# Three issuers for the first stack transfers, and slot reads ahead of weight loads, in an attention and expert kernel

## The chip, the core and the metric

The kernel runs on one core of a Trainium2 chip. The core has five engines with queues of their own: TensorE (PE, with its weight loads shown as PEld), VectorE (DVE), ScalarE (ACT), GpSimd (POOL) and SyncE (SP), which here only issues DMAs. ACT and POOL issue DMAs too. The metric is the device time of one execution in microseconds (us), as the median of several runs.

## What is computed

A gated cross-attention layer, then a mixture of experts in which each token goes to one expert. Batch 4, 512 tokens, width 256, 16 heads of 16; 8 experts of width 1024. All in float32.

```python
def xattn(query, ctx, adj, mask, Wq, bq, ...):        # heads of 16
    scores = einsum('bhqd,bhkd->bhqk', Q, K) / sqrt(16) + adj
    scores = where(mask == 0, -inf, scores)
    out = einsum('bhqk,bhkd->bhqd', softmax(scores), V)
    return out @ Wo.T + bo

x = x + tanh(g_xattn) * xattn(layernorm(x), ctx, ...)
n = layernorm(x)
e = argmax(softmax(n @ gate_w.T))                     # one expert a token
x = x + tanh(g_ffn) * prob[e] * (relu(n @ w1[e] + b1[e]) @ w2[e] + b2[e])
```

## The kernel before, in words

**Attention.** The four batches run one after the other, each in 64 score tiles of 128 queries by 512 keys for one head. `step(b, n)` exists once for each engine, and step n does a little for several tiles: PE makes the scores of tile n (L940); DVE adds the mask and takes the row maximum (L1588); POOL (L682) or, for two of eight tiles and a few at the end, ACT (L1255) negates and shifts; PE transposes tile n-4 (L951); ACT exponentiates it (L1229); PE weighs the values (L963). Score tiles use three PSUM banks (`NS`), their results six SBUF buffers (`NB`), the transposes two PSUM banks (`NTB`). The other work (projections of the next batch, tail of the batch before: heads, turn, out, normed, gate, rank) is dealt to fixed steps by lists such as `LAST_USES`, `SLOT_STEPS` and `TABLE_STEPS`.

**The stack.** Q and K are split into three bf16 parts each, and the eight products that matter are stacked along the partitions, so one bf16 matmul gives a score. `stack_in` (L348 to L356) copies from `parts` into the stack: for each half g and side t (0 is Q, 1 is K), eight DMAs of 64 KB. In batch 0 the stack comes in four groups, m by g, and scores of tiles 0, 8, 16, 24 wait for groups 0 to 3 (`s_first`). SP issues most of them (L400 to L407), ACT five and three of the t=1 ones of groups 0 and 1 (`FIRST_ACT`). While they are under way PE runs filler matmuls (`keep_busy`, L820): 46, then a wait for `s_issued` (SP is through group 0), then 12. All engines work their own queue in order.

**Last batch.** Most tokens' experts are known before the last batch ends, so five "early" slots of 128 tokens are prepared in it. DVE builds a slot table in twelve pieces at `TABLE_STEPS` (expert of a slot in `eid`, its start in `base_i`), POOL writes token numbers to `slot_d` in DRAM (L644). SP then loads the weights w1 of three slots (`early_w1`, L484), waits for POOL's writes and reads the five slots' token lists (L497), then two w2 matrices, rows, and two w2 more. POOL copies the lists (`early_index`, L652) at `INDEX_STEP` and gathers token rows with indirect DMAs: `early_normed(s)` (L658) for the normalised ones, of which slots 0 and 1 at `NORMED_STEPS`, and `early_x(s)` (L665) for the residual ones. A wait in front of them holds up POOL's shifts (L682) behind. After the last step POOL issues the other gathers; PE turns rows (L1029), multiplies w1 (L1041) and w2 (L1063), the first use of w2 waiting for all eight matrices (`r_w2`).

**Late slots.** The other slots run in a loop (L1104, L1127, L1137), after which the kernel ends.

Of the kernel before, what the change touches and what calls it, by code (L numbers as in the profile page):

```python
# [11 lines left out]
ds = bass.ds  # L12
# [10 lines left out]
PAIRS = sum(K_PARTS)  # L23


def build(nc, x, ctx_in, mask, g_xattn, g_ffn, adj, Wq, bq, Wk, bk, Wv, bv, Wo, bo,
# [14 lines left out]
    EARLY = -(-(KNOWN - X * (P - 1)) // P)  # L41
# [7 lines left out]
    NG = H // HG  # L49
# [3 lines left out]
    TPG = QPG * HG  # L53
    TILES = GROUPS * TPG
# [3 lines left out]
    NQ = P // (HG * D)  # L58
# [7 lines left out]
    LP = LE + 1  # L66
    LO = LP + QT
    LAG = LO + 1
    FIRST_ACT = (5, 3, 0, 0)
    ACT_SHIFTS = (3, 6)  # L70
    LAST_ACT_SHIFTS = (60, 63)

# [57 lines left out]
                  if w in ("next q", "next k")}  # L130
    SPLIT_STEPS = {n + 1: use for n, use in CAST_STEPS.items()}
    SLOT_STEPS, SCATTERED_STEP = ((54, 59, 62, 67), (41, 43, 46, 47)), (73, 60)
    TABLE_STEPS = (41, 42, 43, 44, 45, 48, 49, 50, 51, 52, 65, 66)
    INDEX_STEP, NORMED_STEPS = TILES - 5, (TILES - 5, TILES - 2)
    ABS_STEPS = {29: 0, 34: 1, 40: 2, 45: 3}
    SHUT_STEPS = {31: 0, 36: 1, 44: 2, 48: 3}
    FIRST_ABS_STEPS, FIRST_SHUT_STEPS = {1: 2, 4: 3}, {2: 2, 5: 3}
# [27 lines left out]
    with ExitStack() as st:  # L165
# [3 lines left out]
        def sem(name):  # L169
            return st.enter_context(nc.semaphore(name))  # L170
# [79 lines left out]
        least, done, stepd = (sb(n, [P, X]) for n in ("least", "done", "stepd"))  # L250
# [44 lines left out]
        t_x, t_out = ([sem(f"{n}{k}") for k in range(2)] for n in ("t_xres", "t_out"))  # L295
        s_adj, s_perm, s_issued = sem("adj"), sem("perm"), sem("issued")
        s_first = [sem(f"first{g}") for g in range(NG)]
        r_fill, r_filled = sem("r_fill"), sem("r_filled")
        s_eps, t_eps, s_half = sem("eps"), sem("t_eps"), sem("half")
        s_md = [sem("md0"), sem("md1")]  # L300
# [37 lines left out]
            eng.sem_inc(s_waited[eng is nc.vector], 1)  # L338

        FIRST = 16 * 2 * PAIRS  # L340
        STACKED = NQ * FIRST

        def place_of(h):
# [4 lines left out]
        def stack_in(eng, par, t, g, m0, m1, ranks, done):  # L348

            pairs = [(q, k) for q, n in enumerate(K_PARTS) for k in range(n)]  # L350
            for rank in ranks:
                a = pairs[rank][t]
                eng.dma_start(
                    stack[rank:P:PAIRS, par, t, g * HG * EC:(g + 1) * HG * EC].rearrange(
                        "p o (h m) s -> p (o h) m s", m=EC)[:, :, m0:m1].rearrange("p h m s -> p h (m s)"),
                    parts[g * (P // NQ):(g + 1) * (P // NQ), t, a, m0:m1].rearrange("p m s -> p (m s)")).then_inc(done, 16)  # L356
# [15 lines left out]
        def _(sp):  # L372
# [27 lines left out]
            for m in range(EC):  # L400
                for g in range(NQ):
                    for t in range(2):
                        sp.wait_ge(s_parts, 2 * m + t + 1)
                        stack_in(sp, ds(0, 1), t, g, m, m + 1, range(FIRST_ACT[m * NQ + g] if t == 1 else 0, PAIRS),
                                 s_first[m * NQ + g])
                    if (m, g) == (0, 0):
                        sp.sem_inc(s_issued, 1)  # L407
# [42 lines left out]
            for b in range(B - 1):  # L450
                t, par = b * QT, ds((b + 1) % 2, 1)
# [32 lines left out]
            def early_w1(s):  # L484
                u = s % len(ew1)
                e = sp.value_load(eid[0:1, s:s + 1], min_val=0, max_val=X - 1)
                sp.dma_start(ew1[u], w1_v[ds(e, 1)].rearrange("x p k f -> p (x k) f")).then_inc(e_w1[u], 16)

            sp.wait_ge(s_stack, last * STACKED)
            sp.wait_ge(e_eid, 1)  # L490
            sp.wait_ge(s_xT, B * 4)
            for s in range(3):
                early_w1(s)
            sp.wait_ge(r_scat, B * (16 * QT))
            for s in range(EARLY):
                at = sp.value_load(base_i[0:1, s:s + 1], min_val=0, max_val=X * TOK)
                sp.dma_start(slots[:, s], slot_d[ds(at, P), 0:2]).then_inc(e_slots, 16)  # L497
            sp.wait_ge(s_score, last * TILES + 6 * TILES // 8)
            for e in range(X // 2, X, 2):
                load_w2(e)  # L500
# [50 lines left out]
        def _(po):  # L551
# [9 lines left out]
            def norm(b):  # L561
                wait_apart(po, s_mv, b * QT + QT)
                po.tensor_scalar(mv[:, :, 1], mv[:, :, 1], EPS, None, ALU.add).then_inc(s_eps, 1)
                po.wait_ge(s_eps, b + 1)
                po.tensor_tensor(rstd[:], mv[:, :, 1], minus_half[:], ALU.pow).then_inc(s_rstd, 1)
# [10 lines left out]
            n = 5  # L576
# [29 lines left out]
            def mask(b, qt):  # L606

                wait_apart(po, s_penal, b * QT + qt + 1)
                po.tensor_tensor(adjm[:, qt], adjr[:, qt], maski[:, qt].bitcast(F32), ALU.subtract  # L609
                                 ).then_inc(s_adjm, 1)  # L610
# [11 lines left out]
            po.wait_ge(s_adj, 16)  # L622
            for qt in range(QT // 2):
                mask(0, qt)
            norm(1)

            def tail_rstd(b, k):
# [30 lines left out]
            def early_normed(s):  # L658
                if s >= EROWS:
                    wait_apart(po, f_xt, s - EROWS + 1)  # L660
                po.indirect_dma_start(erow[s % EROWS][1], None, xn_d[0:KNOWN],  # L661
                                      bass.IndirectOffsetOnAxis(ap=eidx[:, s:s + 1], axis=0)
                                      ).then_inc(e_row[s % EROWS], 16)

            def early_x(s):  # L665
                if s >= EROWS:
                    wait_apart(po, f_out, s - EROWS + 1)
                po.indirect_dma_start(erow[s % EROWS][0], None, x1_d[0:KNOWN],
                                      bass.IndirectOffsetOnAxis(ap=eidx[:, s:s + 1], axis=0)
                                      ).then_inc(e_x1[s % EROWS], 16)  # L670
# [61 lines left out]
            early_x(0)  # L732
            wait_apart(po, s_osb, B * GROUPS + 2)
            early_normed(3)
            early_x(1)
            early_normed(4)
            early_x(2)
            pairs(B, B)
            for t in range(*RANKED[0]):
                to_slots(t)  # L740
            for k in range(2):
                tail_rstd(B, k)
            for s in range(3, EARLY):
                early_x(s)
            pairs(B, B + 1)
            for t in range(*RANKED[1]):
# [50 lines left out]
        def _(pe):  # L797
# [19 lines left out]
            def keep_busy(n, o=bank[0]):  # L817

                for _ in range(n):
                    pe.matmul(o[:, 0:2 * P], ones[:], ident[:].bitcast(BF16), start=True, stop=True)  # L820
# [148 lines left out]
            def step(b, n, uses, last=False):  # L969

                if n < TILES or not last:
                    if n < NG * TPG and n % TPG == 0 and b == 0:
                        pe.wait_ge(s_first[n // TPG], FIRST)
                    if n == TILES:

                        pe.wait_ge(s_stack, b * STACKED + STACKED)
                    scores(b, ds((b + n // TILES) % 2, 1), n)
                if LT <= n and (n < TILES + LT or not last):
                    transposes(b, n - LT)
                if n >= LP + TPG and (n - LP) % TPG in (0, 2):  # L980
                    g, c = divmod(n - LP - TPG, TPG)
                    if g == 0 and c == 0:
                        pe.wait_ge(s_v, b * 2 + 2)
                    weigh(b, g, c)
                    weigh(b, g, c + 1)
                for i, what, k in at_step(uses, n - 1):
                    if what.startswith("next"):
                        next_rest(b, i, what, k)
                for i, what, k in at_step(uses, n):
                    if what == "heads" and k == 2:  # L990

                        pe.wait_ge(s_osb, b * GROUPS + (NG + 2))
                    if what == "values":
                        values(b, i, k)
                    elif what.startswith("next"):
                        next_use(b, i, what, k, b + 1)
                    else:
                        tail_use(b, i, what, k)
# [3 lines left out]
                next_use(0, first_next(j), what, k, 0)  # L1002
                next_rest(0, first_next(j), what, k)
            pe.wait_ge(s_parts, 2)
            keep_busy(46)
            pe.wait_ge(s_issued, 1)
            keep_busy(12)
            pe.wait_ge(t_ones, 2)
# [143 lines left out]
        def _(act):  # L1152
# [25 lines left out]
            def next_use(b, i, what, k, nxt):  # L1178
                o = sp_bank[i % 2]
                act.wait_ge(s_m, ready(b, i))  # L1180
                if what in ("next x", "next ctx"):
                    dst = xT if what == "next x" else cT
                    act.activation(dst[:, k], o[:], ACT.Copy).then_inc(s_xT, 1)
                    act.wait_ge(s_xT, nxt * 4 + (1 if what == "next x" else 3) + k)
                    act.sem_inc(s_md[i % 2], 1)
                else:
                    t = int(what == "next k")
                    if nxt == 1:
                        for g in range(NG):
                            act.wait_ge(s_first[g], FIRST)  # L1190
                    if nxt > 1:
                        act.wait_ge(s_stack, (nxt - 1) * STACKED)
                    act.activation(parts[:, t, 0, k], o[:], ACT.Identity,
                                   bias=(bqc, bkc)[t][:, k:k + 1]).then_inc(s_p0, 1)
# [619 lines left out]
```

## Time and profile before

| | us |
|---|---|
| median of 3 runs | 548.91 |
| lowest, highest | 548.83, 552.67 |
| the profiled execution: time | 550.53 |
| the profiled execution: span, first to last instruction | 548.5 |
| PE busy | 526.3 |
| DVE, ACT, POOL busy | 302.3, 309.1, 297.9 |

The granted TensorE clock is 0.998 of full over the span. Busy time is a sum over the span; whether an engine's work sets the end must be read from the waits of the stretch in question. Times in the rows below count from the span's first instruction.

### The profile page before, as it was taken

The page shows a single profiled execution, that of the slowest core. Times are in us where ns is not written, and L with a number is a line of the kernel's source. Part 1 is how long each engine was busy: PE and PEld are TensorE (multiplying, and loading weights), DVE is VectorE, ACT ScalarE, POOL GpSimd, SP SyncE. Part 2 cuts the span into 40 slices and gives each one's busy share as a digit, 9 for nine tenths or more (in the row PEclk, how much of TensorE's full clock was granted, in tenths as well). Part 3 has the DMA queues.
Part 4 walks back from the last instruction along what each step waited for, and adds up shares of the span by engine and source line. Part 5 has one row for each costly group of instructions (what it writes and reads, how often), then busy time and mean ns, then how long its engine had stood idle before and what let it go on. Part 6 is the DMA issues. An engine that isn't in the chain of part 4 may idle for free. (4 is left out here: it accounts for less than half of the span.)

```text
span 548.5 us, 13306 instructions
## 1 busy us (share of the span) xinstructions
PE 526.3 (96%) x4123; PEld 405.1 (74%) x4124; DVE 302.3 (55%) x923; ACT 309.1 (56%) x678; POOL 297.9 (54%) x424
## 2 busy tenths in 40 slices
PE   8999999989999999999999999888999999999997
PEld 5577667667666667666676666658899999999996
DVE  2776587976677887668885878845340211111111
ACT  4366678665678665778675676664332333333322
POOL 5346566665567575468574556555244444443451
PEclk9999999999999999999999999999999999999999
DMA  8633625400405510204520057499136665555570
GB/s 288 206 110 132 192 65 183 149 31 6 150 21 192 166 50 1 79 10 153 180 85 1 11 184 250 147 362 320 59 103 218 211 205 196 178 187 184 189 210 1
DMA packets 51489, 77.67 MB, mean 142 GB/s; under 512 B 9945, under 2 KB 34601, under 8 KB 51305
## 3 DMA queue, kind: packets, MB, share of 16 engines
q1 hardware_dynamic: 46600, 67.72, 37.0%
q0 software_dynamic: 4192, 8.73, 5.0%
q8 instruction: 29, 0.48, 0.4%
q10 hardware_dynamic: 640, 0.52, 0.3%
q14 instruction: 28, 0.22, 0.1%
HBM read 52.76 MB, written 8.35 MB: 111 GB/s over the span
## 5 line engine op out<-in xcount | busy, mean ns | idle before, releaser
L1588 DVE CUSTOM_DVE_ANT_0 prob<-bank,adjm 128x512 f32<-128x512 f32 x256 | 172.3, 688 | 70.6 <-issue 39.9
L1229 ACT ACTIVATE pt<-bank 128x512 f32<-128x512 f32 x256 | 152.1, 596 | 87.7 <-PE bank L951 81.2
L682 POOL TENSOR_SCALAR prob<-prob,negmax 128x512 f32<-128x512 f32 x190 | 132.0, 698 | 117.6 <-DVE negmax L1588 113.4
L951 PE MATMUL bank<-ident,prob 128*128 128x128 f32 x1024 | 154.8, 274 | 2.2 <-POOL prob L682 1.3
L951 PEld LDWEIGHTS bank<-ident,prob 128*128 128x128 f32 x1024 | 124.2, 141 | 39.7 <-issue 13.7
L1299 ACT ACTIVATE adjm<-bank,colsm 128x128 f32<-128x128 f32 x184 | 52.6, 368 | 105.0 <-PE bank L1127 80.0
L940 PE MATMUL bank<-w2s 128*128 128x512 bf16 x256 | 97.5, 381 | 8.5 <-DVE negmax L1588 5.7
L963 PE MATMUL bank<-pt,vals 128*32 128x256 f32 x1024 | 68.3, 385 | 0.9 <-DVE vals L1386 0.5
L1127 PEld LDWEIGHTS bank<-xT,pt 128*128 128x128 f32 x576 | 67.1, 192 | 0.9
L1127 PE MATMUL bank<-xT,pt 128*128 128x128 f32 x576 | 67.2, 275 | 0.0
L1137 PE MATMUL bank<-w2s,adjm 128*128 x288 | 65.1, 379 | 0.0
L1137 PEld LDWEIGHTS bank<-w2s,adjm 128*128 128x128 f32 x288 | 53.3, 190 | 6.5
L1255 ACT ACTIVATE prob<-prob,negmax 128x512 f32<-128x512 f32 x66 | 47.4, 719 | 13.7 <-DVE negmax L1588 12.3
L1783 DVE SCALAR_TENSOR_TENSOR cT<-bank,slots,rows 128x256 f32<-128x256 f32 x18 | 8.7, 484 | 72.5 <-PE bank L1137 72.4
L940 PEld LDWEIGHTS bank<-w2s 128*128 128x128 bf16 x256 | 25.5, 100 | 31.3 <-DVE negmax L1588 14.9
L963 PEld LDWEIGHTS bank<-pt,vals 128*32 128x32 f32 x1024 | 27.0, 109 | 22.7 <-issue 9.8
L644 POOL DMA_INDIRECT slot_d<-pair,posi x20 | 20.9, 1046 | 19.3 <-DVE posi L1511 10.0
L1776 DVE SCALAR_TENSOR_TENSOR rows<-maski,slots,rows 128x256 f32<-128x256 f32 x18 | 8.7, 484 | 39.8 <-DMA rows<-x_d,lidx 27.9
L753 POOL COPY lidx<-slots 128x1 int32<-128x1 int32 x18 | 5.1, 283 | 43.4 <-DMA slots<-slot_d 43.2
L767 POOL DMA_INDIRECT out_y<-cT,lidx x18 | 18.3, 1015 | 15.9 <-DVE cT L1783 11.0
L755 POOL DMA_INDIRECT rows<-xn_d,lidx x18 | 18.1, 1005 | 14.3 <-POOL lidx L753 12.7
L609 POOL TENSOR_TENSOR adjm<-adjr,maski 128x512 f32<-128x512 f32 x16 | 20.6, 1285 | 3.1 <-ACT maski L1218 3.1
(195 smaller groups left out, 624.4 us busy)
## 6 DMA issues: line engine op xcount, KB each, us to landing
pt<-in_L_ffn_w SPq DMA_DIRECT2D x19, 1024.0 KB
w2s<-parts SPq DMA_DIRECT2D x96, 128.0 KB
w2s<-in_L_ffn_w SPq DMA_DIRECT2D x8, 1024.0 KB
maski<-in_mask_Bx1xSxS_ik SPq DMA_DIRECT2D x4, 1024.0 KB, 5.6
w2s<-parts SPq DMA_DIRECT2D x56, 64.0 KB, 2.1
xres<-in_x SPq DMA_DIRECT2D x18, 128.0 KB
x_d<-rows SPq DMA_DIRECT2D x18, 128.0 KB
xn_d<-rows SPq DMA_DIRECT2D x18, 128.0 KB
```

The costliest lines, as they stand in the source:

```text
L609: po.tensor_tensor(adjm[:, qt], adjr[:, qt], maski[:, qt].bitcast(F32), ALU.subtract).then_inc(s_adjm, 1)
L644: po.indirect_dma_start(slot_d, bass.IndirectOffsetOnAxis(ap=posi[:, t:t + 1], axis=0), pair[:, t], None, bounds_check=X * TOK - 1, oob_is ...
L682: po.tensor_scalar(prob[:, m], prob[:, m], -1.0, negmax[:, m:m + 1], ALU.mult, ALU.add).then_inc(s_shpool, 1)
L940: pe.matmul(sc_bank[m][:], q, k, start=True, stop=True).then_inc(s_score, 1)
L951: mm = pe.transpose(tr_bank[n % NTB][:, c * P:(c + 1) * P], prob[:, n % TILES % NB, c * P:(c + 1) * P], ident[:])
L963: mm = pe.matmul(pv_bank[32 * j:32 * j + 32, (g % 2) * HALF:(g % 2 + 1) * HALF], vals[:, c, hg * HG + j, :], pt[:, g % 2, c, j, :], start= ...
L1127: mm = pe.matmul(h_bank(u, c), w1s[:, v, k, c * P:(c + 1) * P], xgT[:, u, k], start=k == 0, stop=k == EC - 1)
L1137: mm = pe.matmul(y_bank(u), hT[:, u, c], w2s[:, ds(e, 1), c, :].rearrange("p x e -> p (x e)"), start=c == 0, stop=c == FC - 1)
L1229: act.activation(pt[:, g % 2, :, j, q2 * P:(q2 + 1) * P], tr_bank[c % NTB][:].rearrange("p (c q) -> p c q", c=QT), ACT.Exp).then_inc(s_cac ...
L1255: act.activation(prob[:, m], prob[:, m], ACT.Identity, scale=-1.0, bias=negmax[:, m:m + 1]).then_inc(s_shact, 1)
L1299: act.activation(hT[:, u, c], h_bank(u, c), ACT.Relu, bias=b1c[:, ds(e * FC + c, 1)]).then_inc(f_hT, 1)
L1588: ve.tensor_tensor_reduce(out=prob[:, m % NB], in0=sc_bank[m % NS][:], in1=adjm[:, qt], scale=-1.0, scalar=BIG, op0=ALU.add, op1=ALU.min, ...
```

## The change

`FIRST_POOL = 3`: of group 0's eight t=1 transfers ACT issues 4 (was 5), POOL 3 with a semaphore of its own, and SP 1 (was 3). The first `keep_busy` goes from 46 to 36. In the last batch SP reads the five slots ahead of the three w1 loads. `INDEX_STEP` is one step earlier (58 for 59), the first five `TABLE_STEPS` one later. After the last step POOL gathers `early_normed(4)` ahead of `early_x(1)`, and `early_x(2)` comes behind the two `tail_rstd`.

```diff
-    FIRST_ACT = (5, 3, 0, 0)
+    FIRST_ACT = (4, 3, 0, 0)
+    FIRST_POOL = 3
...
-    TABLE_STEPS = (41, 42, 43, 44, 45, 48, 49, 50, 51, 52, 65, 66)
-    INDEX_STEP, NORMED_STEPS = TILES - 5, (TILES - 5, TILES - 2)
+    TABLE_STEPS = (42, 43, 44, 45, 46, 48, 49, 50, 51, 52, 65, 66)
+    INDEX_STEP, NORMED_STEPS = TILES - 6, (TILES - 5, TILES - 2)
...
+        s_fpool = sem("fpool")
...
+        FIRSTS = [FIRST - 16 * FIRST_POOL] + [FIRST] * (NG - 1)
...
-                        stack_in(sp, ds(0, 1), t, g, m, m + 1, range(FIRST_ACT[m * NQ + g] if t == 1 else 0, PAIRS),
+                        done = FIRST_ACT[m * NQ + g] + (FIRST_POOL if (m, g) == (0, 0) else 0)
+                        stack_in(sp, ds(0, 1), t, g, m, m + 1, range(done if t == 1 else 0, PAIRS),
                                  s_first[m * NQ + g])
...
             sp.wait_ge(s_xT, B * 4)
-            for s in range(3):
-                early_w1(s)
             sp.wait_ge(r_scat, B * (16 * QT))
             for s in range(EARLY):
                 at = sp.value_load(base_i[0:1, s:s + 1], min_val=0, max_val=X * TOK)
                 sp.dma_start(slots[:, s], slot_d[ds(at, P), 0:2]).then_inc(e_slots, 16)
+            for s in range(3):
+                early_w1(s)
...
             for qt in range(QT // 2):
                 mask(0, qt)
+            po.wait_ge(s_parts, 2)
+            stack_in(po, ds(0, 1), 1, 0, 0, 1, range(FIRST_ACT[0], FIRST_ACT[0] + FIRST_POOL), s_fpool)
             norm(1)
...
             early_normed(3)
+            early_normed(4)
             early_x(1)
-            early_normed(4)
-            early_x(2)
             pairs(B, B)
...
-            for s in range(3, EARLY):
+            for s in range(2, EARLY):
                 early_x(s)
...
-                        pe.wait_ge(s_first[n // TPG], FIRST)
+                        pe.wait_ge(s_first[n // TPG], FIRSTS[n // TPG])
+                        if n // TPG == 0:
+                            pe.wait_ge(s_fpool, 16 * FIRST_POOL)
...
             pe.wait_ge(s_parts, 2)
-            keep_busy(46)
+            keep_busy(36)
             pe.wait_ge(s_issued, 1)
             keep_busy(12)
...
-                            act.wait_ge(s_first[g], FIRST)
+                            act.wait_ge(s_first[g], FIRSTS[g])
+                        act.wait_ge(s_fpool, 16 * FIRST_POOL)
```

## Rows read from the trace of the kernel before

**Rows 1.** The page, busy time: us, share of the span, instructions
```profile
PE 526.3 (96%) x4123; PEld 405.1 (74%) x4124; DVE 302.3 (55%) x923; ACT 309.1 (56%) x678; POOL 297.9 (54%) x424
```

**Rows 2.** Windows: stretch, length, busy by engine, clock, DMA share, GB/s
```profile
13.00:20.00 7.00, 6.77 (x16) 2.78 (x16) 3.75 (x6) 5.20 (x9) 3.62 (x5) 1.00 0.82 265
20.00:26.00 6.00, 5.85 (x48) 4.50 (x48) 4.81 (x12) 0.63 (x1) 0.63 (x2) 1.00 0.50 158
...
412.00:545.00 133.00, 132.18 (x906) 124.19 (x906) 18.34 (x38) 46.17 (x162) 57.98 (x70) 1.00 0.54 183
```

**Rows 3.** Timeline to group 1: start, us, engine (q: DMA issue), operation, idle before
```profile
23.80 3.17 SPq L353 DMA_DIRECT2D w2s<-parts  x5
...
20.97 4.35 ACTq L353 DMA_DIRECT2D w2s<-parts  x5
...
21.00 6.50 PE L820 MATMUL bank<-ident,ones 128*128 128x256 bf16 x58 [0.15 <-DVE parts L1669]
...
21.83 0.43 DVE L1667 CAST parts<-rest 128x512 bf16<-128x512 f32 x1
...
25.76 0.24 POOL L563 TENSOR_SCALAR mv<-mv 128x4 f32<-128x4 f32 x1 [5.37 <-DVE mv L1363]
...
27.35 0.38 PE L940 MATMUL bank<-w2s 128*128 128x512 bf16 x1
...
35.58 0.39 PE L940 MATMUL bank<-w2s 128*128 128x512 bf16 x1 [0.91 <-DMA w2s<-parts]
```

**Rows 4.** DMA issues, 12 to 34 and 38 to 46: KB each, us to landing
```profile
w2s<-parts SPq DMA_DIRECT2D x24, 64.0 KB, 2.2
...
xn_d<-atT POOLq DMA_DIRECT2D x1, 1.0 KB, 8.3
...
slot_d<-rows POOLq DMA_DIRECT2D x1, 512.0 KB, 3.2
```

**Rows 5.** Timeline of the last batch near tiles 42 and 48, DVE and PE
```profile
334.42 0.56 DVE L1511 TENSOR_SCALAR posi<-posf,dead 128x4 int32<-128x4 f32 x1
...
335.57 0.69 DVE L1588 CUSTOM_DVE_ANT_0 prob<-bank,adjm 128x512 f32<-128x512 f32 x1 [0.21 <-DVE cmp_t L1531]
...
336.33 0.39 PE L940 MATMUL bank<-w2s 128*128 128x512 bf16 x1 [1.10 <-DVE negmax L1588]
...
344.71 0.39 PE L940 MATMUL bank<-w2s 128*128 128x512 bf16 x1 [0.47 <-DVE negmax L1588]
```

**Rows 6.** Timeline of SP's queue in the last batch
```profile
349.13 0.39 SPq L487 DMA_DIRECT2D adjr<-in_L_ffn_w  x1
...
352.62 4.84 SPq L497 DMA_DIRECT2D slots<-slot_d  x5
```

**Rows 7.** Timeline at the last tiles: POOL, PE and ACT
```profile
361.44 0.19 POOL L655 COPY eidx<-slots 128x5 int32<-128x5 int32 x1 [1.25 <-DMA slots<-slot_d]
...
364.42 0.66 PE L951 MATMUL bank<-ident,prob 128*128 128x128 f32 x4 [0.85 <-POOL prob L682]
...
364.35 0.71 ACT L1255 ACTIVATE prob<-prob,negmax 128x512 f32<-128x512 f32 x1
...
365.11 0.60 ACT L1229 ACTIVATE pt<-bank 128x512 f32<-128x512 f32 x1
```

**Rows 8.** DMA by queue (packets, MB, share) and landing, 348 to 377 us
```profile
q1 hardware_dynamic: 6676, 8.61, 88.0%
q0 software_dynamic: 257, 0.73, 6.8%
...
xcin<-in_L_ffn_w SPq DMA_DIRECT2D x1, 1024.0 KB, 8.9
```

**Rows 9.** Timeline of PE in the first experts
```profile
370.98 1.95 PE L1041 MATMUL bank<-xT,adjr 128*128 128x128 f32 x16
...
377.19 0.41 PE L919 MATMUL bank<-ident,attn 128*128 128x128 f32 x2 [1.90 <-DVE region L1503]
...
382.73 3.62 PE L1063 MATMUL bank<-w2s,adjm 128*128 x16
```

## The prediction

> **What bounds the kernel now.** I read the page first: TensorE (PE) is busy 96% of the span [rows 1]. The windows then say where the other 4% lies [rows 2]. From 412 us on PE is busy 132.2 of 133 us, so the second half of the experts can give nothing; what the change can win lies ahead of it. Two stretches bear on it: the run-up to the first score tile, where PE is "busy" mostly with filler matmuls (L820), and the last batch with the first experts, 330 to 412 us. A filler is busy time that costs what it delays, so for the run-up the timeline counts, not the share.
>
> **Run-up.** The page's chain does not reach back so far, so I read the timeline. PE runs 58 fillers from 21.00 and the first score starts at 27.35 [rows 3]; one filler is worth (27.35 - 21.00)/58 = 0.109 us. Beside them the stack transfers are issued: SP one each 3.17/5 = 0.63 us, ACT five from 20.97 to 25.32 [rows 3]. SP issues eight of t=0 and three of t=1 for group 0; the row of five SP issues in [rows 3] begins with its first t=1 transfer at 23.80, so the third starts at about 25.07 and, with 2.2 us to landing [rows 4], is there at 27.3: fillers and transfers end together. The next gate is group 1: PE idles 0.91 us until 35.58 for its transfers [rows 3]. The list of waits has no other place where PE waits for the stack.
>
> **Change 1, issuers.** Of group 0's eight t=1 transfers ACT now issues 4, POOL 3 and SP 1. SP's ninth starts at 23.80 and lands at 26.0. ACT's fifth issue goes; its fourth starts near 20.97 + 3 x 0.87 = 23.6 and lands at 25.8. POOL waits for the same semaphore, about 20.97, and has been idle for 5.37 us when its next work, the norm of batch 1, starts at 25.76 [rows 3]. No POOL issue stands in that stretch; priced as an SP issue, three end near 22.9, as an ACT issue near 23.6, and nothing is late behind them. Landing of a POOL transfer is the unknown. Rows from both sides: 2.2 us for SP's own 64 KB, 3.2 us for the 512 KB fill of slot_d from POOL, 8.3 us for a 1 KB write from POOL [rows 4], issued near 14 us when the DMA engines were 82% busy [rows 2]. From 20 to 26 us they are 50% busy [rows 2], nearer to the fill's case, so I take 3.2: third issue at 22.3, landed at 25.5.
> The trace shows that DVE's cast of 128x512 takes 0.43 us inside this window [rows 3]. The Trainium skill (SBUF — State Buffer, SBUF: two separate sides) warns that a vector operation in a two-port mode keeps GpSimd from writing the descriptors of its DMAs. By that rule the POOL transfers could slip by that cast, to 25.9 instead of 25.5; no run here shows it yet, and neither landing changes the sum.
>
> PE: 48 fillers instead of 58, so the first score at 21.00 + 48 x 0.109 = 26.25, a gain of 1.1 (the wait on s_issued passes: SP is through its ninth at 24.4, the 36th filler ends at 24.9). What counts is the group 1 gate. SP has two issues fewer ahead of group 1, so 2 x 0.63 = 1.27 us earlier: 35.58 becomes 34.31. PE would be there at 35.58 - 0.91 - 1.10 = 33.57 and waits 0.74. Groups 2 and 3 come from the same stream and move alike. Gain 1.27, carried through the batches, since PE is the bound there and waits for no stack transfer again.
>
> **Change 2, table steps.** Five pieces of the slot table move one step on. Before, the first stands ahead of tile 42 on DVE: posi ends at 334.98, the tile starts at 335.57, and PE loses 1.10 us at 336.33 [rows 5]. Without the piece the tile starts some 0.6 earlier. But all five remain ahead of tile 47, and PE's next wait is for tile 48, 0.47 us at 344.71 [rows 5]; DVE's work up to there is unchanged, so the 0.6 reappears as a longer wait there. Cost 0; bounds -0.6 and +0.3 (one more link).
>
> **Change 3, slot reads ahead of three weights.** Before: three weight loads from 349.13, five slot reads from 352.62 to 357.46, 1.12 apart with their value loads [rows 6], then two w2 loads. Swapped, the slot reads start at 349.13 ahead of all the weights' bytes and are in before 357; the weights start 5 x 1.12 = 5.6 us later, at 354.7. The w2 issues behind them stay, the same eight instructions standing ahead. The weights land late but hidden: the slowest of the three took 8.9 us [rows 8], 5.6 later it is in by 366, and PE uses the first at 370.98 [rows 9].
> POOL's early_index no longer idles 1.25 us for the slots [rows 7], and moved a step ahead, with its gather, it lets tile 61's negation on POOL run some 2 us earlier. PE's 0.85 us wait at 364.42 goes [rows 7]. Does the end of attention follow? ACT works in order: negation of tile 63 (364.35 to 365.06), then tile 61's exponential at 365.11 [rows 7], already right behind. PE's transposes of tile 63 need that exponential's bank, and the last exponential stands behind those. So only 0.05 us is won: the wait moves from tile 61's to tile 63's transposes, since the ACT negation is next in line.
>
> What is paid: the DMA stream. Between 348 and 377 us 8.61 MB move on q1 and 0.73 on q0 [rows 8]; w2 needs 3 w1, 4 w2, two xres and four row stores ahead of or with it, 8.12 MB of q1, so it is complete just before 377. PE first reads it at 382.73 [rows 9]. The stream started near 350.9 (an estimate: 1.8 us behind its first issue, a little under the 2.2 us that a small one takes to landing; rate 9.34/26.1 = 0.358 MB/us) and will start 5.6 later, 356.5. Seven gathers (0.92 MB) now fall before its end: 9.04/0.358 = 25.3, so 381.8. By plain shift, 377 + 5.6 + 0.5, 383.1. PE's need of 382.73 lies between: cost 0 to 0.4. I take 0, the byte count being the nearer reckoning. The x-row loads and stores slip by the same 5.6 and are used from 380 on.
>
> **Change 4, gathers.** early_normed(4) goes ahead of early_x(1), and early_x(2) behind tail_rstd, with some 1 us of POOL each. early_x(2) is then issued near 385 and used near 403; POOL meanwhile passes the pairs' wait, which DVE sets, no earlier. 0.
>
> Sum: -1.27 + 0 - 0.05 + 0 + 0 = -1.3 on a span of 548.5. That execution took 550.5 in all; the median of the runs is 548.9, and I set the same difference against it: 547.6.
>
> **Rivals.**
> A, forecast: 547.6, own range 547.0 to 548.2.
> B, the waits in the last batch are real gains too: PE's 0.85 and DVE's 0.6 both count, 547.6 - 1.4 = 546.2. Or the stranger 1.90 us wait at 377.19 [rows 9], in which DVE, ACT and SP all got PE's signals late in the midst of the full DMA stream, does not recur: 545.7. For it: the waits are in the rows; against the first: ACT's row right behind.
> C, w2 late: if gathers and stream slow each other, complete by 383.7 or later, 1 us or more given back, 548.6. It decides once w2 lands past 382.7; nothing lies behind it to absorb it, since PE is full to the end.
> D, the start gains nothing: three issuers slow each other. ACT's five issues beside SP's took 4.35/5 = 0.87 us each against SP's 0.63 [rows 3], so issuers do cost each other. If SP's nine lose 9 x 0.14 = 1.27 us to the third issuer, group 1 is no earlier: 548.9.
> E, the other side: POOL's transfers land late. By the 8.3 us row the third is there at 22.3 + 8.3 = 30.6. From the first score to group 1 PE needs 34.67 - 27.35 = 7.32 us, so group 1 starts at 37.9 instead of 35.58: +2.3, 551.2. It eats into the gain from a landing at 27.0 on and makes the kernel slower from 28.3. Half-way between the two rows, 5.7 us (28.0), the gain would be 0.3. The Trainium skill (DMA: Bandwidth & Descriptors, Anatomy of one DMA — SWDGE (gpsimd) path) gives about 2.0 us plus bytes/436e3, an estimate of 24.5 for this landing; the 8.3 us row here does not agree with it, the slot_d row nearly does, and by it the sum stays.
>
> **Chances.** A 0.50, B 0.18, C 0.10, D 0.12, E 0.10. The range reaches from B's far case, 545.7, toward E, which is mostly left out, with C and D inside and a little for a median of few runs: 545.7 to 549.6. About 1% (5.5 us) is what a measurement of this kernel can tell from no change; only several cases together or something unseen get there: faster 0.04, same 0.94, slower 0.02.
>
> **What would show it.** First score at 26.2 to 26.3, POOL's transfers with 3 us to landing, a shorter wait ahead of group 1 at 34.3: right. First score past 27: D or E, told apart by SP's and POOL's issue rows. A wait at PE's first L1063 matmul: C. PE's waits near tiles 45 and 48: 0.5 and 1.1 instead of 1.1 and 0.5 if step 2 is right. L951 without its 0.85 wait, but another ahead of tile 63's transposes, and the last exponential no earlier relative to tile 60's transposes: step 3. Wrong would be a gain over 2 us with all of it after 330 us.

## The result, and the profile after

In the first comparison, four runs of each kernel, the changed kernel took 555.63 us in the median (552.88 to 557.54) and the kernel before 549.31: ratio 1.0104, 95% interval 1.0073 to 1.0135. Forecast were 547.6 and a gain of 0.2%. The square brackets behind a ratio are its 95% interval from here on. Against many more runs the changed kernel came out at 1.0025 [1.0004, 1.0046] and 1.0027 [1.0005, 1.0049] in two further comparisons (12 runs against 35 each). So the sign of the loss is firm and its size is not; both figures are taken up below. The profiled execution has a span of 550.9 us, 2.4 more than before.

The page after, busy time, which answers [rows 1]:

```profile
PE 527.8 (96%) x4113; PEld 404.6 (73%) x4114; DVE 303.1 (55%) x923; ACT 308.8 (56%) x678; POOL 299.4 (54%) x427
```

The windows after (stretch, length, busy time of PE, PEld, DVE, ACT and POOL with instructions, granted clock, DMA share, GB/s), for [rows 2] and the last batch:

```profile
20.00:26.00 6.00, 5.85 (x49) 4.50 (x48) 5.25 (x13) 0.69 (x1) 2.25 (x5) 1.00 0.70 175
...
350.00:357.00 7.00, 6.68 (x55) 4.43 (x50) 6.33 (x19) 4.93 (x10) 2.79 (x5) 1.00 0.11 5
357.00:384.00 27.00, 23.86 (x204) 18.44 (x204) 13.28 (x52) 14.41 (x38) 14.08 (x20) 0.94 1.03 361
412.00:545.00 133.00, 132.08 (x907) 123.86 (x906) 17.87 (x37) 46.88 (x165) 57.29 (x70) 1.00 0.57 183
```

The same two stretches of the last batch in the kernel before:

```profile
350.00:357.00 7.00, 6.07 (x48) 3.96 (x46) 6.39 (x20) 4.49 (x8) 3.70 (x7) 1.00 0.89 311
357.00:384.00 27.00, 23.16 (x209) 18.70 (x210) 12.92 (x48) 14.10 (x37) 14.05 (x20) 1.00 0.99 339
```

From 412 us on nothing has changed. Between 350 and 357 the DMA engines, which carried 311 GB/s before, now carry 5. That hole is the slot reads' place in SP's queue, and all the weight bytes stand behind it.

**The run-up.** Timeline after, for [rows 3]:

```profile
22.62 2.16 SPq L356 DMA_DIRECT2D w2s<-parts  x2
...
22.33 2.46 ACTq L356 DMA_DIRECT2D w2s<-parts  x2
...
21.27 1.63 POOL L356 DMA_DIRECT2D w2s<-parts  x3 [0.84 <-DVE parts L1677]
...
27.71 0.38 PE L945 MATMUL bank<-w2s 128*128 128x512 bf16 x1 [1.27 <-DMA w2s<-parts]
...
34.87 0.38 PE L945 MATMUL bank<-w2s 128*128 128x512 bf16 x1
35.50 0.63 PE L956 MATMUL bank<-ident,prob 128*128 128x128 f32 x4 [0.25 <-ACT pt L1237]
```

POOL's transfers among the DMA issues of 20 to 34 us after (KB each, median us to landing), beside [rows 4]:

```profile
w2s<-parts POOLq DMA_DIRECT2D x3, 64.0 KB, 3.0
```

POOL's three issues take 1.63 us and land 3.0 us later in the median, near the 3.2 reckoned, but the third, the one that counts, takes 4.00 and is in at 26.39 instead of 25.5. Two issues of SP take 2.16 us and two of ACT 2.46. The fillers end at 26.4, and PE then idles 1.27 us for SP's ninth transfer, issued at 23.29 and landed at 27.62: 4.33 us, where the sum had 2.2. So the first score (the matmul of the first score tile) is 0.36 later than before instead of 1.1 earlier. Group 1 is no longer waited for, but right behind it PE waits for ACT (pt at 35.50).

**The last batch.** SP's queue after, for [rows 6]:

```profile
350.20 4.86 SPq L499 DMA_DIRECT2D slots<-slot_d  x5
355.83 0.40 SPq L491 DMA_DIRECT2D adjr<-in_L_ffn_w  x1
...
358.57 5.54 SPq L475 DMA_DIRECT2D w2s<-in_L_ffn_w  x2
364.15 4.14 SPq L414 DMA_DIRECT2D xres<-in_x  x2
...
370.87 3.62 SPq L475 DMA_DIRECT2D w2s<-in_L_ffn_w  x2
```

The timeline of POOL and PE, for [rows 7, 9]:

```profile
359.74 0.19 POOL L661 COPY eidx<-slots 128x5 int32<-128x5 int32 x1
...
366.02 0.63 PE L956 MATMUL bank<-ident,prob 128*128 128x128 f32 x4 [0.47 <-ACT pt L1237]
...
367.78 3.51 PE L968 MATMUL bank<-pt,vals 128*32 128x256 f32 x32 [0.20 <-issue]
...
377.29 0.41 PE L924 MATMUL bank<-ident,attn 128*128 128x128 f32 x2 [0.28 <-DVE region L1511]
...
384.12 1.13 PE L1070 MATMUL bank<-w2s,adjm 128*128 x4 [1.12 <-issue]
...
413.72 0.44 PE L1111 MATMUL bank<-ident,rows 128*128 128x128 f32 x2 [0.59 <-DMA rows<-xn_d,lidx]
```

A window of PE at the end of attention, columns as above:

```profile
368.00:371.00 3.00, 3.00 (x32) 1.63 (x24) 0.30 (x2) 0.00 (x0) 0.00 (x0) 0.50 1.09 355
```

POOL no longer waits for the slots. PE waits 1.12 us ahead of the first w2 matmul; by the landings in the trace the last w2 byte is in at 383.92, before at 377.18. The 32 matmuls that weigh the values and end attention (L968) take 3.51 us, 1.93 in the profile of e13, because the granted clock is 0.50 from 368 to 371: the 1.2 GHz level. PE had been busy but for waits of 0.2 to 0.5 us before it fell.

### The profile page after: what moved, and what is told of

Same layout as the page of the kernel before. It is cut to its first block and busy times, and to the rows that moved or that the text cites. A ratio compares the mean times of both kernels' runs of the same rounds, so it can differ in the third digit from the quotient of the medians.

```text
span 550.9 us, 13291 instructions
## 1 busy us (share of the span) xinstructions
PE 527.8 (96%) x4113; PEld 404.6 (73%) x4114; DVE 303.1 (55%) x923; ACT 308.8 (56%) x678; POOL 299.4 (54%) x427
## 5 line engine op out<-in xcount | busy, mean ns | idle before, releaser
L968 PE MATMUL bank<-pt,vals 128*32 128x256 f32 x1024 | 69.9, 392 | 0.9 <-DVE vals L1394 0.5
L945 PEld LDWEIGHTS bank<-w2s 128*128 128x128 bf16 x256 | 25.5, 100 | 31.3 <-issue 15.8
L968 PEld LDWEIGHTS bank<-pt,vals 128*32 128x32 f32 x1024 | 27.7, 110 | 23.2 <-issue 10.6
L766 POOL DMA_INDIRECT rows<-x_d,lidx x18 | 17.2, 954 | 10.0 <-DVE cT L1791 5.2
```

The costliest lines, as they stand in the source:

```text
L945: pe.matmul(sc_bank[m][:], q, k, start=True, stop=True).then_inc(s_score, 1)
L968: mm = pe.matmul(pv_bank[32 * j:32 * j + 32, (g % 2) * HALF:(g % 2 + 1) * HALF], vals[:, c, hg * HG + j, :], pt[:, g % 2, c, j, :], start= ...
```

## The experiments

Eighteen profiles of these kernels (both kernels, their repeats and the versions below) share most of their path, so steps are compared across all of them. Whole times are compared only within a set: versions that ran side by side, with runs of the kernel before among them. That matters here: the kernel before took 549.69 us in the median among e1 to e4, 553.87 among e5 to e7, 552.72 with c1 and 551.99 with c2. Where two versions of one set are compared below, the difference is of their means, and the figure behind ± is its 95% interval, worked out from the single times.

**e1: the run-up's change alone.** Kernel before with

```diff
-    FIRST_ACT = (5, 3, 0, 0)
+    FIRST_ACT = (4, 3, 0, 0)
+    FIRST_POOL = 3
...
-            keep_busy(46)
+            keep_busy(36)
```

> The kernel before with the run-up of the change alone (4 issues on ACT, 3 on POOL, 1 on SP, 36 filler matmuls). Theory S (the slot swap makes it slow): this one is no slower than before, 0 to 1 us faster: first score near 27.7 as in the changed kernel, group 1 near 34.9, no clock drop near 368, no wait at the first L1070 matmul. Theory R (the run-up is what costs): 3 to 6 us slower than before.

Measured: 1.0024 [1.0010, 1.0038]. In place of the expected gain of 0 to 1 us that is a loss of 1.3 us, much less than the 3 to 6 us of the other theory. First score 27.31, tile 8 at 34.49, but tile 16's exponential only 0.24 us earlier than before, and this profile has the clock at its lower level from 365.3 to 368.7. Over all profiles, the exponential of tile 16 starts at 52.80 to 54.43 us in the eleven kernels with three issuers (mean 53.46, standard deviation 0.50) and at 53.26 to 53.84 in the seven with two (mean 53.56, 0.19). The third issuer gains nothing that these show, and the spread is wider with it.

**e2 and e12: the slot reads ahead of the weights, alone.**

```diff
-            for s in range(3):
-                early_w1(s)
             sp.wait_ge(r_scat, B * (16 * QT))
             for s in range(EARLY):
...
+            for s in range(3):
+                early_w1(s)
```

and INDEX_STEP one earlier.

> The kernel before with the slot reads ahead of the weights and INDEX_STEP one step earlier, nothing else. Theory S: 3 to 6 us slower than before (about 1%), w2 complete near 384 us, a wait of 1 to 3 us at the first w2 matmul of the early slots, and a stretch at half clock near 365 to 372. Theory R and theory T (table steps): as before within 1 us.

> The kernel before with the slot reads ahead of the weights and the index computation one tile earlier, again, now beside the changed kernel. Theory that the slot reads are the whole loss of the change but for some 0.1%: within 0.2% of the changed kernel. Rival, that run-up and table steps add their own 0.25% each, as each showed alone: 0.3 to 0.5% below the changed kernel.

Measured: e2 1.0073 [1.0046, 1.0100], e12 1.0008 [0.9989, 1.0028] (mean 0.95 ± 1.01 us below c2, so within the expected 0.2%, with the rival's 0.3% not excluded). PE's timeline at the first w2 matmul in e2, and the window behind it:

```profile
384.69 1.70 PE L1063 MATMUL bank<-w2s,adjm 128*128 x6 [3.42 <-issue]
```

```profile
386.00:389.00 3.00, 3.00 (x9) 2.35 (x8) 0.00 (x0) 0.00 (x0) 0.00 (x0) 0.50 1.03 395
```

and the timeline of e12:

```profile
377.40 0.41 PE L919 MATMUL bank<-ident,attn 128*128 128x128 f32 x2 [1.90 <-DVE region L1503]
...
383.70 1.56 PE L1063 MATMUL bank<-w2s,adjm 128*128 x6 [0.59 <-issue]
```

w2 lands at 384.49 and 383.51, 7.3 and 6.3 us later than before. In e2 PE pays 3.42 us, and 1.7 more for the clock, which fell to the 1.2 GHz level at 386.0, after that wait. In e12 it pays 0.59: PE was already held up 1.90 us at 377.40, the wait that [rows 9] show. So how much of the late weights is felt depends on what else has delayed PE. The same edit measured 0.7% in one set and 0.1% in another; that this is the reason is argued from one profile of each.

**e3: table steps later and gathers moved.**

```diff
-    TABLE_STEPS = (41, 42, 43, 44, 45, 48,
+    TABLE_STEPS = (42, 43, 44, 45, 46, 48,
```

> The kernel before with the five table steps one later and the moved gathers, nothing else. Theory T (DVE's work near tiles 42 to 48 costs): 1 to 3 us slower, with a long DVE copy near 340. Theory S: within 0.5 us of before.

Measured: 1.0025 [1.0011, 1.0038]; e4 below, which has this edit too, 1.0013. That is the 1 to 3 us slower of the first theory. The profile has no wait for w2 (landed 378.42, needed 381.27). The exponentials of tiles 38 and 50 lie 16.69 us apart, before 16.25.

**e4: the changed kernel without the slot swap.** SP's order and INDEX_STEP as before.

> The changed kernel with the weights again ahead of the slot reads and INDEX_STEP as before. Theory S: 0 to 1 us faster than before. Theory R or T: nearly all of the changed kernel's loss of 4 to 6 us remains.

Measured: 1.0013 [0.9999, 1.0027], against 1.0073 for e2 beside it. Here w2 lands at 378.71 and PE does not wait. In this set the swap is the larger part of the loss: e2's mean is 3.6 ± 1.4 us above e4's. But e4 was not faster than before, as expected, and it holds the edits of e1 and e3 together, which measured 0.24% and 0.25% alone. So these two figures do not add up, and neither is much above what such a set can tell.

**e5 and e10: one megabyte less ahead of w2.** The changed kernel with the third early w1 transfer behind the second pair of w2:

```diff
-            for s in range(3):
+            for s in range(2):
                 early_w1(s)
...
             for e in range(X // 2 + 1, X, 2):
                 load_w2(e)
+            early_w1(2)
```

> The changed kernel with the third early weight load moved behind the second pair of w2 loads; the slot reads stay first. Theory S (w2 comes late because 3 MB of weights start 5.6 us later ahead of it): 1 MB less ahead of w2, so w2 is complete near 381 and the wait at the first w2 matmul is gone; 2 to 4 us faster than the changed kernel, within 0.3% of before. Theory Q (it is the clock or the gathers, not the order of the bytes): as slow as the changed kernel, 1.007 or more of before.

> The changed kernel with the third early first-layer transfer behind the second pair of second-layer transfers, again, now beside the changed kernel itself on one chip. Theory of the late weights: 0.7 to 1.2% below the changed kernel, and between 0.4% below and 0.1% above the kernel before. Rival, that the changed kernel loses by its run-up and table steps: within 0.3% of the changed kernel.

**c1: the changed kernel itself, beside e8 to e10.**

> The changed kernel itself once more, as the control for its neighbours on the same chip. If its loss is its own (the slot reads put 3.1 MB of first-layer weights beside the second-layer weights, which land at 383.9 us of its profile and not at 377.2): slower than the kernel before by 0.7 to 1.1% here too, and by as much than the version with the third early first-layer transfer behind the second pair of second-layer transfers. If the first comparison was a matter of that chip: within 0.3% of the kernel before.

Measured: e5 0.9969 [0.9949, 0.9989], e10 0.9984 [0.9965, 1.0003], c1 1.0025 [1.0004, 1.0046]. The mean of e10 is 552.04, of c1 554.01: 1.97 ± 0.99 us, or 0.36%, for moving one transfer. Both expectations had the changed kernel's loss at 0.7% or more, as in the first comparison; c1 shows 0.25%, within the 0.3% of its rival, and e10's gain is half of what was expected, its interval reaching into the 0.3% of the rival. The timeline of PE in c2 (the second repeat of the changed kernel; c1 waited 1.59), then in e10:

```profile
384.12 1.12 PE L1070 MATMUL bank<-w2s,adjm 128*128 x4 [1.90 <-issue]
```

```profile
381.66 1.95 PE L1049 MATMUL bank<-xT,parts 128*128 128x128 f32 x16
383.45 1.89 PE L1071 MATMUL bank<-w2s,adjm 128*128 x8
```

In e10 the w2 matmul follows without a wait; w2 is in at 381.87. Nothing else was touched, and the changed kernel is then no slower than the kernel before: this pair, with e13 and e11 below, carries the mechanism. The two profiles alone would not. Their first w2 matmuls start together (383.40 in c1, 383.45 in e10), since e10 ended attention 1.15 us later. And moving the transfer may be worth something by itself, as e9 shows next.

**e8 and e9: the same on the kernel before,** e8 with the slot swap, e9 without.

> The kernel before with the slot reads ahead of the early first-layer weights and the index computation one tile earlier, and with the third early first-layer transfer (1 MB) moved behind the second pair of second-layer transfers. Theory that the bytes ahead of the second-layer weights are the loss: those weights land 2.7 to 3 us earlier than with the slot reads alone (384.5 us), so by about 381.7, the 3.42 us wait ahead of the first second-layer matmul is gone, and the time is within 0.3% of the kernel before, against 0.73% above it for the slot reads alone. Theory that the slot reads cost by something else (the queue of SP held up, the earlier index computation): still 0.5 to 0.8% slower.

> The kernel before, with nothing but the third early first-layer transfer moved behind the second pair of second-layer transfers. Theory that in the kernel before the weights are in time as they stand (landed 377.2 us, used first at 382.73 with no wait): within 0.2% of before. If instead the lighter stream is what made two versions of the changed kernel 0.3 to 0.45% faster than before: faster by 0.3% or more here too.

Measured: e8 0.9987 [0.9967, 1.0008], e9 0.9979 [0.9955, 1.0002]. The slot swap costs nothing that the runs show once w2 is in time (380.58): e8's mean is 0.6 ± 1.0 us above e9's. And e9 has no swap and yet POOL does not wait for the slots, as its timeline shows:

```profile
359.27 0.57 POOL L633 TENSOR_TENSOR rstd<-mv,minus_half 128x1 f32<-128x1 f32 x1
359.79 0.19 POOL L656 COPY eidx<-slots 128x5 int32<-128x5 int32 x1
```

With two weight loads ahead of the slot reads instead of three, these are early enough. I had expected e9 to be equal to before within 0.2%; its point value is just there, and the interval does not tell it from a small gain. If that gain is real, a part of e10's 1.97 us could have the same source. Against it speaks that what e9's profile gains, POOL's wait for the slots, is gone in the changed kernel already, and that the waits for w2 which e10 removes (1.12 to 1.90 us in the four profiles with them) are of the size of its gain. No run separates the two.

**e7: fillers in place of the wait,** 24 of them ahead of PE's wait for w2 in the changed kernel, to keep the clock up.

> The changed kernel with 24 filler matmuls (2.6 us of PE) ahead of the wait for w2. Theory S with an idle-bound clock: the wait is filled, no half-clock stretch follows the w2 wait, mean granted clock of the runs 0.998 or more, time 0 to 1 us less than the changed kernel. If the clock falls for another reason: clocks of 0.994 to 0.996 as in the changed kernel, and time equal or up to 1.5 us more.

Measured: 0.9995 [0.9973, 1.0017]. PE's timeline:

```profile
383.04 2.78 PE L825 MATMUL bank<-ident,ones 128*128 128x256 bf16 x24
385.66 1.68 PE L1072 MATMUL bank<-w2s,adjm 128*128 x7
```

The clock stayed at 1.00 from 384 to 390, but the fillers ran 1.2 us past w2's landing (384.45), and part of the price only changed its name. The mean granted clock of its runs, 0.9984, is where it was expected, but e5 and e6 beside it, without the fillers, have 0.9976 and 0.9979. Whether e7 beats the changed kernel can't be said, since the two were not in one set. It is slower than moving the transfer: e5, beside it, is 1.4 ± 0.8 us below it.

**c0: the kernel before, a second profile.**

> The kernel before, unchanged, for a second profile. If the 1.90 us wait behind the first rank matmuls belongs to the kernel it is there again; if it was of that one execution, about 0.3 us stand there, the first w2 matmul starts near 381, and about 0.5 to 0.9 us of wait stand at the first late gather instead.

Measured: 552.69 us with a span of 550.7. The 1.90 us wait is there again (1.96), so it is not of one execution. The 2.2 us over the first profile are spread: run-up 0.25, 0.4 more to the last exponential (POOL's wait for the slots is 2.09 instead of 1.25), 0.5 between there and the late rows, and 1.0 behind the late rows.

**c2, e11, e6 and e13: what the table steps cost inside the change.** e11 is the changed kernel with the old TABLE_STEPS (five steps differ), e6 and e13 (one kernel, run twice) have the late third transfer besides.

> The changed kernel itself, a second control. If the kernel before takes 549 to 550 us on this chip, 0.7 to 1.0% above it (second-layer weights landed at 383 to 384 us, 1.1 to 1.6 us of wait, and a stretch at half the clock in some executions). If the kernel before takes 552 us or more, as in the two last sets, 0.2 to 0.4% above it, since those executions lose clock in both kernels.

> The changed kernel with nothing but the six table steps back at tiles 41 to 45. In four profiles with the steps moved and the slot reads ahead, the exponentials of tiles 38 to 50 of the last batch lie 16.94 to 16.96 us apart, in six with the old steps 16.24 to 16.28. Theory that this is on the path: those 16.25 us again, and the kernel 0.5 to 0.7 us (0.1%) faster than the changed one. Rival, that the weights land no earlier for it, so that what the tiles give back is waited out ahead of the second-layer matmuls: the wait there grows by as much, and the time is the same within 0.05%.

> As e5_w2first, and the table steps where they were before. Theory T2 (the table steps one later put a COPY on VectorE beside a slot scatter on GpSimd, +0.4 to 0.7 us between tiles 38 and 50): 0.4 to 0.7 us faster than e5_w2first, at or under before (0.998 to 1.001). If the steps cost nothing: equal to e5_w2first.

> The changed kernel with the third early first-layer transfer behind the second pair of second-layer transfers and the old table steps, the version that came out 0.45% faster than the kernel before on one chip. Theory that it is better by what its profile shows (no wait of GpSimd for the slots, 0.9 us of its path; weights in time): 0.1 to 0.4% faster than the kernel before here too, and 0.6% or more below the changed kernel. Rival, that its lead came from executions in which the kernel before lost clock: within 0.15% of the kernel before.

Measured: c2 1.0027 [1.0005, 1.0049], e11 1.0017 [0.9996, 1.0038], e6 0.9955 [0.9937, 0.9974], e13 0.9981 [0.9962, 1.0000]. Moving the transfer is seen again: e13's mean is 2.09 ± 0.93 us below e11's. The old table steps are not seen in whole times: e11 is 0.91 ± 1.15 us below c2, and e6 0.16 ± 0.83 below e5, where 0.4 to 0.7 was expected. They are seen in every trace. From tile 38's exponential to tile 50's it takes 16.94 to 16.95 us in the six profiles with the new steps and the slot swap, 16.69 and 16.72 in e3 and e4 without the swap, and 16.24 to 16.29 in the ten with the old steps. In e11 the wait for w2 is still 1.65 us, so what the tiles give back may be waited out there, as its rival had it. The timelines of DVE, PE and POOL in the changed kernel:

```profile
339.50 1.20 DVE L1549 COPY end<-end 128x2 f32<-128x2 f32 x1
...
342.02 0.42 DVE L1410 TENSOR_TENSOR attn<-bank,rinv 128x256 f32<-128x256 f32 x1
342.59 0.17 DVE L1549 COPY end<-end 128x4 f32<-128x4 f32 x1
342.79 0.16 DVE L1550 TENSOR_TENSOR end<-end 128x4 f32<-128x4 f32 x1
...
342.65 0.41 PE L924 MATMUL bank<-ident,attn 128*128 128x128 f32 x2 [0.90 <-DVEq L1414]
...
339.31 1.36 POOL L688 TENSOR_SCALAR prob<-prob,negmax 128x512 f32<-128x512 f32 x2
```

and in e11:

```profile
338.67 0.32 DVE L1549 COPY end<-end 128x2 f32<-128x2 f32 x1
...
337.99 1.02 POOL L650 DMA_INDIRECT slot_d<-pair,posi  x1 [0.17 <-issue]
339.06 0.70 POOL L688 TENSOR_SCALAR prob<-prob,negmax 128x512 f32<-128x512 f32 x1
```

A copy of two numbers a partition takes 1.20 us and ends at 340.70, as POOL's two negations end (339.31 + 1.36 = 340.67); in e11 it ends at 338.99 and POOL's instruction at 339.01. One step later, the small table operations begin just after a negation has begun. The Trainium skill (SBUF — State Buffer, SBUF: two separate sides) says that a vector operation in a two-port mode or with two SBUF inputs and a GpSimd operation take a shared pair of ports as an exclusive lock, and the later one blocks until the other's instruction ends. The trace agrees in that the copy ends within 0.03 us of an instruction of POOL in both places; whether the copy ran in such a mode it doesn't tell. By that rule one negation would have to be sat out. In the changed kernel it is two, back to back (339.31 to 340.67); in e3 the same copy takes 0.52 us and ends with the first of them. In addition a second table piece now shares a tile with rinv and attn of the row before it, so PE's transposes of attn wait.

## Why the prediction was wrong

By its own steps, on the profiled execution (span 548.5 to 550.9):

**Run-up, forecast -1.27.** Failed. POOL's landing was near (3.0 us in the median, 4.00 for the third; rival E did not occur, since 26.39 is still ahead of the 27.0 from which it would have eaten into the gain). The first score was forecast from a landing of SP's ninth transfer at 26.0; the median of 2.2 us was taken for it, and it took 4.33. For group 1, what failed is "SP has two issues fewer ahead of group 1, so 2 x 0.63 = 1.27 us earlier", in two places. ACT's and SP's issues were priced by their means, and a pair of SP's took 2.16 us and a pair of ACT's 2.46 beside a 16 KB instruction fetch that the trace shows at 23.0 to 23.9 us (in the kernel before at 22.05 to 23.4, with one issue of 1.46 on ACT and one of 1.15 on SP beside it); that is a coincidence in time, not a tested cause. And a gate that goes was taken as time won: behind it ACT's pace holds PE (the wait for pt at 35.50), so of 0.7 to 1.1 us at tile 8 there are -0.2 to +0.6 left at tile 16's exponential (six profiles: after, c2, e1, e4, e11, e13; mean 0.1). Rival D has the outcome. Its reason, three issuers slowing one another evenly, the issue times do not show, since most of SP's stay at 0.6 us; the landings of the transfers issued from 21 to 24 us, 2.6 to 4.3 us against 2.1 to 3.2 before, leave room for it.

**Table steps, forecast 0, bounds -0.6 and +0.3.** Failed in sign and size: +0.7 in the changed kernel (16.95 from tile 38 to 50, against 16.24 before and 16.29 in e11), +0.45 in e3. "DVE's work up to there is unchanged" was true of the instructions and false of their durations. The first wait shrank as said, from 1.10 to 0.40 us (at 335.83), but the 0.6 did not reappear ahead of tile 48, where the wait is 0.47 as before and not 1.1: a new one of 0.90 came ahead of the attn transposes, and one of 0.22 behind it.

**Slot reads and the end of attention, forecast -0.05.** Right in what it names: the wait at tile 61 is gone, and one of 0.47 for ACT stands ahead of tile 63's transposes. The size the profiles do not resolve: with the old table steps, from tile 38's exponential to the last, six profiles with the swap have 32.65 to 33.40 us (mean 33.08), the two of the kernel before 33.06 and 33.46, a mean of 33.26. The 0.2 us between the means is less than what profiles of one kernel differ by.

**w2, forecast 0 (0 to 0.4).** This is the failed step that matters: the term was put at nothing, because w2 was reckoned complete ahead of PE's need. Rival C named the late landing, with a chance of 0.10 and a price of 1 us. The reckoning had w2 complete at 381.8. SP's first slot read began at 350.20 and not at 349.13, since it stands behind the table: 0.67 of that is the table steps, which e11 gives back (15.47 us after tile 38's exponential, in the changed kernel 16.14). That puts the stream 1.1 later. And it took 26.3 us instead of 25.3 (357.6 to 383.9). Together 383.9, past the need of 382.73. The rate was not at fault, 0.369 MB/us against the 0.358 reckoned, and so C's reason, gathers and stream slowing each other, is not what the trace shows. The count of bytes was short: 9.71 MB moved in that stretch and not 9.04, 8.75 instead of 8.12 of them on q1, and the next w1 load is issued at 377.72, 6 us ahead of w2's last byte. The DMA view of 357.63 to 383.92 after:

```profile
DMA packets 6359, 9.71 MB, mean 369 GB/s; under 512 B 348, under 2 KB 5212, under 8 KB 6356
...
q1 hardware_dynamic: 5992, 8.75, 95.0%
```

The plain shift, 383.1, which I set aside for the byte count, was the nearer one, and with the shift as measured it is right: the first weight load is issued 6.70 us later than before, and w2 lands 6.74 later (c1 6.16 and 6.03, c2 6.78 and 6.75, e11 5.79 and 5.51, e12 5.84 and 6.33, e2 6.36 and 7.31, all against the first profile of the kernel before). The cost on PE was 1.12 us in this profile, 1.59, 1.90 and 1.65 in c1, c2 and e11, and 2.0 and 2.1 us in the runs of e10 against c1 and of e13 against e11 (± 1 us each).

**The 1.90 us wait at 377.19.** It did not recur in the changed kernel: 0.28, with 0.60 and 0.55 in c1 and c2. It stands in five of the eighteen profiles (the kernel before twice, e8, e9, e12), each time with DVE and ACT getting PE's signals late and in a burst: in the kernel before four signals of PE come between 376.41 and 376.59, for matmuls that had run between 373 and 375. A burst of the same kind, but earlier, stands in eight more profiles, where the wait is 0.52 to 0.67 us; the five without any burst have 0.28. All five with the long wait have two issuers in the run-up, two other such kernels (e2, e3) are without it. It was not a gain all the same: without it PE is 1.6 us earlier at the first w2 matmul if w2 is there, and in all twelve profiles without it and without e7's fillers PE waits 0.5 to 1.0 us for the late row gathers (0.59 above), where those with it wait 0 to 0.25. What delays the signals stays open.

**Clock, not foreseen.** In five of eighteen profiles the clock is at the 1.2 GHz level for 3.41 us between 365 and 390 us, which costs 1.6 to 1.7 (3.51 against 1.93 above). The kernel e9, near to before, is among them, so the change is not its only condition. Over the 98 runs of the kernel before in the last three sets, 0.001 less of mean granted clock goes with 0.43 us more (a correlation; in the first set, where its clock hardly varies, there is none). The changed kernel's four first runs had 0.994 to 0.996, the kernel before among e1 to e4 0.9995: by that slope (an estimate) some 2 of the 5.7 us, and less on the later occasions, where the kernel before loses clock too.

Sum for the profile: run-up +0.2 (last batch begins at 283.75, before 283.55), table +0.7, the rest of attention -0.7 (last exponential 367.08, before 366.92), clock +1.6, w2 +1.1, the missing wait -1.6, the smaller waits around it +0.1, late gathers +0.8 (w2 matmul to late rows 29.60, before 28.76), end +0.2: +2.4, as the spans have it. Forecast was -1.3: the 1.27 of the run-up was not there, and w2, table and clock were not in it. What stays open is the size of the loss where the kernel before runs at 549 us, 0.25% or 1.0%: the repeats, with more runs, favour the lower, but in both of them the kernel before was at 552 us or more. The late weights account for some 2 us of it by the runs; the rest of the first comparison's 5.7 us is given to the clock only by the estimate above, and is not shown.

## What to carry to other kernels

A transfer that is moved ahead of a full stream moves the stream: work out where its last byte lands by the shift and by the bytes, with those that are issued behind it and move before it is complete, and take the later one where the need is as near as here, 1 us. Then cut bytes ahead of the deadline rather than reorder: the version with one load moved behind w2 and the old table steps measured 0.9955 [0.9937, 0.9974] as e6 and 0.9981 [0.9962, 1.0000] as e13, and by the means it is 0.30 and 0.23% faster than the kernel before. Before a gate is counted as won, look for what stands just behind it, here ACT. And small operations of VectorE that are moved by one step should be laid against GpSimd's instructions of that step, since each can wait out a whole one, here even two.

## What the hardware showed

- An issue on SP is not always short. In the last batch, with the DMA share at 1.03 (357 to 384 us), the sixth w2 issue, at 359.08, took 5.02 us (0.84 before), and the residual read (xres) behind it 3.40. The last w2 issue came 7.8 us later than before, where the first weight issue had come 6.7 later. What holds such an issue the trace doesn't tell.
- A DVE copy of two to four numbers a partition takes 0.17 us alone and 0.32, 0.52 or 1.20 beside POOL's instructions.
- A transfer of 64 KB issued by POOL costs 0.51 to 0.58 us of issue and lands 2.6 to 3.0 us later (medians of five profiles; single ones to 4.00), issued by SP 2.1 to 2.5 in the median (single ones to 4.33).
- The same run-up code came to tile 16's exponential at 53.06 us in c1 and at 54.43 in e7: with three issuers its start differs by 1.4 us from one execution to another, with two (seven profiles) by 0.6.
